# A two-layer kernel on one core: the dense part's squares move from ScalarE to GpSimd, and the hand-written order of pieces is another one

## The chip, the core and the metric

The kernel runs on one core of a Trainium2 chip. The metric is the device time of one execution in microseconds (us), smaller is better. Engines are named as in the profile: PE is TensorE (PEld its weight loads), DVE VectorE, ACT ScalarE, POOL GpSimd, SP SyncE.

## What is computed

The input x is 4 batches of 512 tokens with 128 features, all float32. Two layers, each a LayerNorm and two branches that read it:

```
xn = layernorm(x)
x  = x + L0_attn(xn) + L0_ffn(xn)      # 16 heads, attention over the feature axis;
                                       # 64 experts of width 88, top 8 per token, and 2 shared ones
xn = layernorm(x)
x  = x + L1_attn(xn) + L1_ffn(xn)
```

`L1_attn`: queries and values are relu(xn @ enc); for every token the distances to the 64 tokens behind it are taken per head, the nearest 32 of them are kept with exp(-distance) as weights, and their values are summed; a decoder matmul follows. `L1_ffn`, called the dense part here, is

```
h = xn @ Wfc.T + gate * (xn @ v.T @ fast_b.T @ u.T)     # 128 -> 512
r = max(h, 0)
out = (r * r) @ Wproj.T                                 # 512 -> 128
```

## The kernel before

Every engine has its own program, made of pieces. A piece is a Python generator step; each kind of piece has a letter, and the table `ORDER` writes out for each engine in which order the letters come. `weave` walks through that string. So the order of work on an engine is fixed by hand, and what an engine waits for is set by the semaphores that the pieces name. An engine never passes a piece that waits.

The kinds that matter here:

- `e` on PE: the expert products. The experts' weights are cut into 46 blocks of 128 rows for each batch, 184 in all (n = 0 to 183). Block n fills bank G0 or G1 and bank U0 or U1 (n even or odd), three matmuls each. ACT takes the silu of G; DVE multiplies by U (`S<-S,bank_U`, letter `e` on DVE); the router's weight is put on by DVE for even n (`S<-Rb,bank_G`, letter `m` on DVE, which also frees bank G) and by POOL for odd n (`S<-S,Rb`). `m` on PE is the down product of block n, summed up in bank A.
- ACT makes the high part of each weight block (`Whi`), POOL the low part (`Wlo`).
- `y` and `a`: router and attention of layer 0. `h`: layer 1's head, from the sum of experts (`mo`, copied by ACT from bank A when the 46 down products of a batch are in) through LayerNorm (`yn`), the transposes, the encoder, the metric (`met`) and the lengths of queries and keys (`nmx`, `pq`).
- `d` on PE, `k` (keys, `Ra`) and `n` (near) on ACT: the distances of a group of 64 tokens (8 groups g0 to g7 to a batch) and their exponentials, in tile `Ed`. `k` on DVE: the choosing of the nearest 32 by four rounds of MAX8 and MATCH_REPLACE8. `q` on POOL: subtraction and scaling of what was chosen (`Wk`, `Wm`). `t` on PE: turning that tile (L825), the weighted sum of values, and the decoder. `g` on DVE and ACT: the gathering behind them. In the last batch these matmuls use banks G and U, and the last group is cut in two halves, which DVE finishes alone.
- `f` on PE: one 128-token tile of the dense part's up product, into bank X0, 16 tiles in all (line 670). `f` on ACT (line 1496): relu from the bank into one half of `PR`, then the square in place. `v` on PE (line 682): the down product of the tile, into bank A; it waits on the semaphore `ffsq`. As bank A belongs to the experts until the last batch's sum is copied, all 16 `v` pieces come behind that.

Since there are two halves of `PR`, the relu of tile i waits for the down product of tile i - 2 (`ff2_tile`); since there is one bank X0, the up product of tile i + 1 waits for the relu of tile i.

Of the kernel before, what the change touches and what calls it, by code (L numbers as in the profile page):

```python
# [7 lines left out]
ALU = mybir.AluOpType  # L8
# [41 lines left out]
        "eeemmteeteaeeemmesmtestmesemteeeetmestmmeeeememeeeemmeeeetemeamthmmteeeeeamtheatmaehtaeeeteatemmamee"  # L50
        "meheemhheeeemeemmhehmehaekeekmeedeadeedmememamdeamdeeetfemtdefeemmdeemmfeteetdemeeeeeemteememeetmete"
        "mmetmeetmeeeetmmeeetemtmeeetmeemetmmeeeeeemmtmmthvtvvtfhthfthvhvhfhhhvkddkxdfvfvddtvfvtddtvfdtfvfvfv"
        "vfttvttvtxfttfvttvtvxttxtttttt",
    "dve":
        "yyycyyyyyyyyyyeycyyyyyyeayyyayyyyyyeecyyyyeeyamyeemamaemeemaaeuuaumeuemeuuauuuuemeaemeyeymeeyyyyyyym"
        "eeyyyyyymeeyyymeyeyymeemeyyyyemeeyymeemeemeemeemeemeeeemeeyymeehhyyyymheyyeyyyhhmeeymyeyyhyeyyyyymeh"
        "hehhmeyehmehehahmeahemekkkemkkkkakekekakkmekkekkmgekeamagekmaeekkgkmkegekkemekekmkagekkgemekkekkgkmk"
# [1 line left out]
        "kakaemeakkegkkmeekmekkakkakemeekagkmeekkmgekkkkkmeeakkeakgmeekkgmekgkkemeekkkkmeekmeekgeemeaghhghehh"
        "ameemgeaemgeahgaemeaaemehhhehahmehehmehhemeekkakmekkakkemkkegkkmeekkkekkkmeekmegkekmkegkekmkekgkekme"  # L60
        "gekkmegekkkmegkmekkeemegkkemeekgkkhhhghhghghhhhhhhhhkkkkkkkkkkkkkkkkkkgkkkkkkkkgkkkkgkgkkkkkkgkkgkkk"
        "kkkgkkgg",
    "act":
        "yxxyxyeexexcexxecayaxesyxxseexesaexesxxxeeaxexaeaexxuxeeuxeuuyuxyexeexxeexxxeexexexexexexyexseeyxees"
        "xxxsexeexxxeexexexexexexesxeyxxemeyexexxxexehxeexhehexxoohxeheehhxyexxexhexhhkkveevxknxknenkaeexnaxk"
        "nnxkenxgexeakxnneexxngexeexxexexngnexegxexeaxxexeexegaaxxegxeexexexesxxseexesymesegxxxyexhygexhexhox"
        "eoexexexhheehhxeyxxhhehxekxekexvnkvexnnankaxxnnxkenekkageexxkxenenxgeexxneaxxeexaenaneexxgexxexesxgs"
        "esxeexxgexexexexexesxeexxmgehxeexxghaeaxgeexxhaexeooxhexehaxehheexhxxhhaevxkvkeenkxxnenanekxxknneken"
        "kgfxxkexfenxnexgenexxexeexxexnexgneegxexxeexxeegxxeegxxexeeemgfhghfhohhfhofhhhhkkvnnnnkfnnfvkkfnnnnf"
        "gkkfnnnnkgffnnfffqgfgfqgfgfqgggq",  # L70
    "pool":
        "llylllllalmmlllmaaaclacalamlllmalmllmllmyylmlllmllmllmllmlymlllmmllmlllmlllmllmllmllmlylylmlllmllmll"
        "mhllmlymhlllmllmlmllmlaqllmqallaamqllamplalamlqllmlmlmqlplalmllqmlqlmllmlpmllqllmllmylylplmlhllmlmly"
        "mhllllmmllllaqllaammlaqmlmlalaqlalmlapmllqmlqlmllmllqmplllmlqmllmlmllqllpmlllmlamplhlaaamallaalmlmha"
        "lllmlmllmllqmlllqlmlqmllmlplmqlllmqmlllpmllqmllmqmlllpmmqphhhqqqqqqqq",
# [1791 lines left out]
```

## Time and profile before

| | us |
|---|---|
| median of 3 runs | 679.48 |
| lowest and highest run | 678.58, 680.74 |
| the profiled execution's own time | 678.06 |
| its span in the trace | 676.3 |
| PE, DVE, ACT, POOL busy | 638.7, 545.1, 444.6, 365.4 |

The span is what the trace shows from the first instruction to the last; 1.8 us of the execution's own time lie outside it. The execution that was profiled is 1.4 us quicker than the median run. Busy times of PE are modelled from the starts of its matmuls, since they are pipelined. All times below count from the start of the span.

### The profile page before, as it was taken

What the parts mean: (1) busy time and instruction counts of PE and PEld (TensorE: products, weight loads), DVE (VectorE), ACT (ScalarE), POOL (GpSimd) and SP (SyncE); (2) the same over time, 40 slices, a digit from 0 to 9 for tenths busy, and PEclk for the clock granted to TensorE, in tenths of its full rate; (3) what the DMA queues carried; (4) which work ended last, traced back from release to release, by engine and by line L of the source; (5) the groups of instructions that cost most, each with busy time, mean ns of one, the idle gap of its engine ahead of it and who ended that gap; (6) DMA issues with size and microseconds to landing.
All of it is one profiled execution on the core that took longest, in us unless ns stands there. A gap on an engine that the chain in (4) does not pass through costs nothing.

```text
span 676.3 us, 14256 instructions
## 1 busy us (share of the span) xinstructions
PE 638.7 (94%) x4792; PEld 430.7 (64%) x4792; DVE 545.1 (81%) x2461; ACT 444.6 (66%) x802; POOL 365.4 (54%) x448
## 2 busy tenths in 40 slices
PE   4887999999999999999999999999999999998886
PEld 3544766667656666767567567666567776675675
DVE  5987778645975999997976899965485999967997
ACT  3674454646787957448587786455888956467953
POOL 2278366566462787665452886653763576621220
PEclk9999999999999999999999999999999999999999
DMA  8940000000000000000000000000000000000000
GB/s 297 392 131 1 0 1 0 1 0 1 0 1 1 2 2 1 1 1 1 2 0 2 2 1 2 1 1 1 1 1 1 2 1 1 1 1 17 18 18 17
DMA packets 12968, 15.81 MB, mean 23 GB/s; under 512 B 1728, under 2 KB 10832, under 8 KB 12384
## 3 DMA queue, kind: packets, MB, share of 16 engines
q1 hardware_dynamic: 12896, 14.91, 6.3%
q8 instruction: 38, 0.62, 0.4%
q14 instruction: 34, 0.28, 0.1%
HBM read 13.85 MB, written 1.05 MB: 22 GB/s over the span
## 4 chain that ended last, share of the span: by engine, by line
PE 61%; DVE 24%; ACT 7%; POOL 4%; issue 3%; DMA 0%; DVEq 0%; POOLq 0%; ACTq 0%
PE bank_A L522 17%; PE bank_U L522 14%; PE bank_G L522 14%; PE bank_X L522 14%; DVE Wk L1278 6%; DVE m L1275 5%; DVE S L859 4%; DVE GWk L859 2%; POOL PR L1654 2%; ACT L1350 1%; PE bank_X L531 1%; ACT Ed L1345 1%; PE bank_X L825 1%; ACT PR L1345 1%; ACT L1345 1%
## 5 line engine op out<-in xcount | busy, mean ns | idle before, releaser
L1654 POOL TENSOR_TENSOR Wlo<-Wgu,Whi 128x256 fp32r<-128x256 f32 x184 | 134.9, 743 | 119.5 <-ACT Whi L1345 116.5
L522 PE MATMUL bank_A<-S,WdT 128*128 128x512 f32 x346 | 172.2, 599 | 0.2 <-POOL S L1654 0.2
L1654 POOL TENSOR_TENSOR S<-S,Rb 128x512 f32<-128x512 f32 x84 | 108.6, 1294 | 72.0 <-DVE S L859 71.4
L859 DVE TENSOR_TENSOR S<-S,bank_U 128x512 f32<-128x512 f32 x173 | 116.6, 684 | 37.5 <-PE bank_U L522 23.3
L1345 ACT ACTIVATE Whi<-Wgu 128x256 fp32r<-128x256 f32 x184 | 73.0, 413 | 53.0 <-PE bank_U L522 48.5
L522 PE MATMUL bank_G<-xH,Whi 128*128 128x512 f32 x184 | 94.7, 515 | 8.0 <-POOL Wlo L1654 3.8
L522 PE MATMUL bank_U<-xH,Whi 128*128 128x512 f32 x184 | 93.4, 508 | 1.6 <-DVE wT L859 1.1
L522 PEld LDWEIGHTS bank_A<-S,WdT 128*128 128x128 f32 x346 | 61.7, 189 | 34.6 <-issue 21.4
L1278 DVE MATCH_REPLACE8 Wk<-m,Wk 128x79 f32<-128x79 f32 x384 | 82.2, 226 | 0.0
L1345 ACT ACTIVATE bank_G<-bank_G 128x512 f32<-128x512 f32 x83 | 48.4, 583 | 42.9 <-PE bank_G L522 42.6
L1345 ACT ACTIVATE S<-bank_G 128x512 f32<-128x512 f32 x90 | 53.7, 596 | 34.3 <-PE bank_G L522 27.5
L859 DVE TENSOR_TENSOR S<-Rb,bank_G 128x512 f32<-128x512 f32 x83 | 56.4, 680 | 22.5 <-ACT bank_G L1345 17.6
L522 PE MATMUL bank_U<-xH,Wlo 128*128 128x512 f32 x184 | 72.9, 396 | 0.0
L522 PE MATMUL bank_G<-xH,Wlo 128*128 128x512 f32 x184 | 72.9, 396 | 0.0
L522 PE MATMUL bank_G<-xL,Whi 128*128 128x512 f32 x184 | 72.8, 396 | 0.0
L522 PE MATMUL bank_U<-xL,Whi 128*128 128x512 f32 x184 | 72.7, 395 | 0.0
L1275 DVE MAX8 m<-Wk 128x8 f32<-128x79 f32 x384 | 63.9, 228 | 0.0
L522 PEld LDWEIGHTS bank_G<-xH,Whi 128*128 128x128 f32 x184 | 34.7, 189 | 34.7 <-issue 17.2
L522 PEld LDWEIGHTS bank_U<-xH,Whi 128*128 128x128 f32 x184 | 34.7, 189 | 23.8 <-issue 8.9
L1345 ACT ACT_TABLE_LOAD x38 | 48.8, 1283 | 0.7
L1350 ACT ACT_TABLE_LOAD x35 | 44.9, 1283 | 6.5 <-DVE mv L926 4.4
L1654 POOL TENSOR_TENSOR Wk<-Ed,Wk 128x316 f32<-128x316 f32 x31 | 26.8, 863 | 37.1 <-DVE Wk L1278 36.9
(294 smaller groups left out, 1176.0 us busy)
## 6 DMA issues: line engine op xcount, KB each, us to landing
Wgu<-in_Wgu SPq DMA_DIRECT2D x2, 2048.0 KB, 14.4
xs<-in_x SPq DMA_DIRECT2D x4, 256.0 KB, 6.0
wqk<-in_w_qkv SPq DMA_DIRECT2D x1, 1024.0 KB, 6.9
Wgu<-in_Wgu SPq DMA_DIRECT2D x1, 1024.0 KB, 9.5
out<-xs SPq DMA_DIRECT2D x3, 256.0 KB, 2.3
Wgu<-in_Wgu SPq DMA_DIRECT2D x1, 512.0 KB, 4.7
wout<-in_w_out SPq DMA_DIRECT2D x1, 512.0 KB, 8.1
wvT<-in_wvT SPq DMA_DIRECT2D x1, 512.0 KB, 9.2
```

Of the source, the lines that this page charges most:

```text
L522: return engine.matmul(dst, lhsT, rhs, start=start, stop=stop)
L531: p = engine.transpose(t[0:rows, 128 * i:128 * i + 128], src3[:, i, :], ident)
L825: p = engine.transpose(t[:, 128 * i:128 * i + 128], Wm[s][:, i, :], ident)
L859: return engine.tensor_tensor(dst, a, b, op)
L1275: top[i] = own(engine.max(w8[:, i, 8 * r:8 * r + 8], v[:, i, :]))
L1278: p = engine.match_replace(wk[:, i, :], w8[:, i, 8 * r:8 * r + 8], v[:, i, :], TAKEN)
L1345: return engine.activation(dst, src, f, bias=bias, scale=scale, accum_out=acc)
L1350: engine.preload_act_table_set(LNEXP)
L1654: return engine.tensor_tensor(dst, a, b, op)
```

## The change

Two things. The square of the dense part (`r * r`) is no longer a second ACT instruction behind the relu but a POOL multiply of `PR` with itself, in place, a new kind of piece on POOL with the letter `f`. It waits until ACT's relu has emptied the bank, and counts `ffsq` up. And the strings of `ORDER` for PE, DVE, ACT and POOL are others from the stretch in which batch 0's sum of experts ends; what stands before is the same, and each letter occurs as often as before (POOL's 16 `f` are new).

```diff
@@ ORDER
-        "mmeeeemeeemeeeemyemesmeeseememeemsmeemeeeemeemeeeemmsemeeeememeemeeeemyemeymmeemeeeehymeeeemmmemeeme"
+        "mmemeeeeeememmememyeeeeesmememeeemsmeesmeeemeeeeseeemeeeeememmeememeeeyeeymemeeymeehmmemmemeememehe"
...
@@ scalar_engine, dense(b)
                     if b * NT + i >= 2:
                         sc_.wait_ge("ff2_tile", b * NT + i - 1)
-                    a = emptied(act(r, t[:, :], ACT.Relu), "ff1", b, i)
-                    sc_.wait_ge(*a)
-                    act(r, r, ACT.Square).then_inc(sems("ffsq"), 1)
+                    emptied(act(r, t[:, :], ACT.Relu), "ff1", b, i)
@@ gpsimd_engine
+            def squares(b):
+                for i in range(NT):
+                    r = PR[:, 512 * (i % 2):512 * (i % 2) + 512]
+                    yield
+                    po.wait_ge(empty(bank("ff1", b, i)), nth("ff1", b, i) + 1)
+                    tt(r, r, r, ALU.mult).then_inc(sems("ffsq"), 1)
...
-            weave("pool", c=zeros(), l=splits(), m=tiles(), y=every(route), a=every(attend), h=every(head), q=every(weights), p=adds())
+            weave("pool", c=zeros(), l=splits(), m=tiles(), y=every(route), a=every(attend), h=every(head), q=every(weights), p=adds(), f=every(squares))
```

**Place 1, DVE, near the end of batch 0's experts** (blocks 24 and 25). `GWk`, `sfc` and `m8r` are tiles of batch 1's router. Before:

```order
L1043 TENSOR_REDUCE GWk<-GWk 128x32 [waits dve]
L863 TENSOR_SCALAR GWk<-GWk 128x32 [waits dve]
L859 TENSOR_TENSOR S<-Rb,bank_G 128x512 [waits down,silu]
L859 TENSOR_TENSOR S<-S,bank_U 128x512 [waits U0_filled,G0_emptied]
L859 TENSOR_TENSOR S<-S,bank_U 128x512 [waits U1_filled,G1_emptied]
L859 TENSOR_TENSOR sfc<-sfc,GWk 128x256 [waits dve]
```

After:

```order
L1043 TENSOR_REDUCE GWk<-GWk 128x32 [waits dve]
L863 TENSOR_SCALAR GWk<-GWk 128x32 [waits dve]
L859 TENSOR_TENSOR sfc<-sfc,GWk 128x256 [waits dve]
L859 TENSOR_TENSOR S<-Rb,bank_G 128x512 [waits down,silu]
L859 TENSOR_TENSOR S<-S,bank_U 128x512 [waits U0_filled,G0_emptied]
```

The router's `sfc` multiply has moved ahead of the weight piece that frees bank G0.

**Place 2, PE, the end of the last batch's experts.** `bank_A<-S,WdT` is a down product, L825 turns the last batch but one's group, `cst,mo` are the transposes of the finished sum. Before:

```order
L522 MATMUL bank_A<-S,WdT 128x512 [waits U0_emptied]
L522 MATMUL bank_A<-S,WdT 128x512 [waits tw_p]
L825 MATMUL bank_X<-cst,Wm 128x128 [waits chosen_p,X2_emptied]
L825 MATMUL bank_X<-cst,Wm 128x128 x3
L531 MATMUL bank_X<-cst,mo 128x128 [waits mo,X1_emptied]
```

After:

```order
L522 MATMUL bank_A<-S,WdT 128x512 [waits U0_emptied]
L825 MATMUL bank_X<-cst,Wm 128x128 [waits chosen_p,X2_emptied]
L825 MATMUL bank_X<-cst,Wm 128x128 x3
L522 MATMUL bank_A<-S,WdT 128x512 [waits tw_p]
L522 MATMUL bank_X<-wT,V 32x32 [waits X2_emptied]
L522 MATMUL bank_X<-wT,V 32x32 x15
L531 MATMUL bank_X<-cst,mo 128x128 [waits mo,X1_emptied]
```

The turn stands before the last down product now, and the sum of values that belongs to it before the transposes.

**Place 3, ACT and POOL, the last batch's first groups.** ACT after the change, from the first keys to the second group's near piece (before, the near pieces of g0 and g1 stood directly one behind the other, behind the `V` copy, and only then came a `Ra` and a dense tile):

```order
L1345 ACTIVATE Ed<-bank_G 128x316 [waits looked,G0_filled]
L1345 ACTIVATE Ed<-Ed,cst 128x316 [waits G0_emptied]
L1345 ACTIVATE Ed<-Ed 128x316 [waits act] x2
L1345 ACTIVATE Ra<-Pk 16x316
L1345 ACTIVATE V<-bank_U 128x512 [waits U1_filled]
L1345 ACTIVATE Ra<-Pk 16x316 [waits G1_filled]
L1345 ACTIVATE PR<-bank_X 128x512 [waits ff2_tile,X0_filled]
L1345 ACTIVATE Ra<-Pk 16x316 [waits G0_filled]
L1345 ACTIVATE PR<-bank_X 128x512 [waits ff2_tile,X0_filled]
L1345 ACTIVATE Ed<-bank_G 128x316 [waits looked]
```

POOL after the change in the same stretch, with the squares:

```order
L1652 TENSOR_TENSOR hg<-hg,kp 128x128 [waits X2_emptied]
L1652 TENSOR_TENSOR PR<-PR 128x512 [waits X0_emptied] x2
L1732 COPY kp<-kp 128x63 [waits X1_emptied]
L1652 TENSOR_TENSOR PR<-PR 128x512 [waits X0_emptied]
L1652 TENSOR_TENSOR hg<-hg,hf 128x512 [waits hf_inv]
L1652 TENSOR_TENSOR PR<-PR 128x512 [waits X0_emptied]
L1652 TENSOR_TENSOR hg<-hf,kp 128x512 [waits U0_emptied]
L1652 TENSOR_TENSOR PR<-PR 128x512 [waits X0_emptied] x2
L1652 TENSOR_TENSOR Wk<-Ed,Wk 128x316 [waits taken]
```

On ACT six other pieces now stand between the near pieces of g0 and g1, and on POOL the squares stand between the head's multiplies and the groups' `Wk` and `Wm`.

## Rows read from the trace of the kernel before

**Rows 1.** The page: busy time by engine, and the chain that ended last.

```profile
PE 638.7 (94%) x4792; PEld 430.7 (64%) x4792; DVE 545.1 (81%) x2461; ACT 444.6 (66%) x802; POOL 365.4 (54%) x448
PE 61%; DVE 24%; ACT 7%; POOL 4%; issue 3%; DMA 0%; DVEq 0%; POOLq 0%; ACTq 0%
```

**Rows 2.** Busy time of each engine in three stretches.

```profile
core 0: us, PE busy (x) PEld busy (x) DVE busy (x) ACT busy (x) POOL busy (x), PEclk, DMA share, GB/s
105.00:596.60 491.60, 487.36 (x3456) 321.42 (x3457) 401.49 (x1800) 334.63 (x595) 295.83 (x362) 1.00 0.01 1
596.60:620.30 23.70, 22.04 (x257) 16.41 (x255) 12.40 (x44) 18.20 (x37) 4.80 (x6) 1.00 0.04 13
620.30:671.60 51.30, 41.84 (x671) 34.96 (x669) 50.86 (x414) 35.64 (x72) 11.01 (x14) 0.97 0.06 16
```

**Rows 3.** Timeline of PE: start, duration, line, tiles [idle before].

```profile
104.89 0.50 PE L522 MATMUL bank_G<-xH,Whi 128*128 128x512 f32 x1 [1.16 <-DVE S L859]
```

**Rows 4.** Timeline of DVE around the same moment.

```profile
104.16 0.68 DVE L859 TENSOR_TENSOR S<-Rb,bank_G 128x512 f32<-128x512 f32 x1
...
106.07 0.42 DVE L859 TENSOR_TENSOR sfc<-sfc,GWk 128x256 f32<-128x256 f32 x1
```

**Rows 5.** The chain that ended last: start, duration, what.

```profile
592.26 0.70 PE bank_U L522 x3
...
596.65 0.61 ACT mo L1345
...
598.02 0.89 PE bank_A L522 x8
...
601.48 0.44 PE bank_X L825 x4
601.92 0.89 PE bank_X L522 x8
602.81 0.45 PE bank_X L531 x4
...
606.45 0.61 ACT Qb L1345
607.06 0.15 ACT hb L1345
...
611.98 1.13 PE bank_U L522 x2
...
615.09 1.09 PE bank_A L522 x8
...
617.41 0.87 PE bank_G L522 x33
```

**Rows 6.** Timeline of DVE in the last batch.

```profile
601.32 1.12 DVE L864 TENSOR_SCALAR mo<-xs,mv,ln 128x128 f32<-128x128 f32 x4
...
612.42 0.51 DVE L864 TENSOR_SCALAR mk<-kp,met 128x575 f32<-128x575 f32 x1
...
620.36 0.67 DVE L1275 MAX8 m<-Ed 128x8 f32<-128x79 f32 x4 [2.59 <-ACT Ed L1345]
...
626.40 0.66 DVE L1275 MAX8 m<-Ed 128x8 f32<-128x79 f32 x4
...
671.17 0.32 DVE L859 TENSOR_TENSOR Wm<-Wk,sm 128x158 f32<-128x158 f32 x1
```

**Rows 7.** Timeline of ACT in the last batch.

```profile
618.30 0.43 ACT L1345 ACTIVATE Ed<-bank_G 128x316 f32<-128x316 f32 x1 [0.26 <-PE bank_G L522]
...
619.36 0.96 ACT L1345 ACTIVATE Ed<-Ed 128x316 f32<-128x316 f32 x2
```

**Rows 8.** Instructions on tile PR: nanoseconds, shortest, median and longest; first and last start.

```profile
L1345 ACT ACTIVATE PR<-PR x20: 629/631/634, 46.8 to 662.0; 128x512 f32<-128x512 f32 x20
L1654 POOL TENSOR_TENSOR PR<-PR x4: 1042/1042/1043, 47.5 to 481.7; 128x512 f32<-128x512 f32 x4
L1654 POOL TENSOR_TENSOR PR<-PR,z x4: 1271/1287/1602, 48.6 to 482.8; 128x512 f32<-128x512 f32 x4
L1654 POOL TENSOR_TENSOR z<-PR x4: 1310/1318/1769, 52.7 to 486.1; 128x512 f32<-128x512 f32 x4
```

**Rows 9.** Groups of POOL's instructions in the last 79 us: count, busy us, mean ns.

```profile
L1654 POOL TENSOR_TENSOR Wk<-Ed,Wk 128x316 f32<-128x316 f32 x8 | 6.9, 858 | 32.6 <-DVE Wk L1278 32.6
L1654 POOL TENSOR_TENSOR Wm<-Wk,sm 128x316 f32<-128x316 f32 x8 | 5.7, 714 | 3.9 <-PE bank_U L825 3.4
```

More of the change, by code:

```diff
@@ L45 @@
         "yeyeyeeemeeaeaemaayeeaseeeseeameesmaeesemmmemmeeeemeemumaeeaeeaumeeeueaueemyeeymmmymeeeeemmeeemmeeee"
-        "mmeeeemeeemeeeemyemesmeeseememeemsmeemeeeemeemeeeemmsemeeeememeemeeeemyemeymmeemeeeehymeeeemmmemeeme"
-        "mheeheeeehmeehhmmeeymeemhmhmeeheeeakeekadeademdeeemeaemmdeadeematmeeteadmeedememmtedteeeemeetmmeeete"
-        "mtmmeteemmeetemmmeeeemteaeeetmmtameaeeeteetememameemmseeeeesmeeseeetseeemhtmytmeeetymmtemhteheyeeemm"
-        "emeheemememhheeemyehemhmheaeeaeeeemkdekedaedeemeadeammdaedateeeteemmmmedemmeetmmeeetdeeeemmeateamema"
@@ L50 @@
[L50 to L53, printed above, removed]
+        "mmemeeeeeememmememyeeeeesmememeeemsmeesmeeemeeeeseeemeeeeememmeememeeeyeeymemeeymeehmemmemeemememehe"
+        "ememheememeeeehmeehhemeyememahheaehmeeeeedkdaeedemmmmaeeedaedemkateeeatdmedemtmetememeemdeeeemteteee"
@@ new lines @@
+        "tmmemmeetemteemememeatmeeeeateateetmmteemeeeeemmeemtemeeatmmseeseeeheemsmtesemeyteymemteeeyehmetheee"
+        "mheemmhheeemmmmeeeheehmeemeheeeeykedmadeadeaeeamdaemdkatmaeeedeetemmmmeemdmtmeetmeeeeeedeemaemaeeeam"
+        "tmememeaeteeeemsmeeetseemmsteetmsmeemeetmeeememeeeetmemetemathmatmeeteaetamheehteaeeetmaetaemememmht"
+        "eeeemhheeemmemaheehmaheememedeedeeeaedeemmeedkmmdeemadkeetfmefeetdfmmeetmeeeteedememmteeeemmmeeeemme"
+        "temteeteetemeemmeeemteeeeteetemetmmeeeetmmtmmmtmthvtvthfhfthvhhvvhhhfvddfkdvfxvkdfdtvtdvtdtdfvfvfvfv"
@@ L54 @@
+        "vttxttfvtfvfttvttvtvxttxtttttt",
     "dve":
         "yyycyyyyyyyyyyeycyyyyyyeayyyayyyyyyeecyyyyeeyamyeemamaemeemaaeuuaumeuemeuuauuuuemeaemeyeymeeyyyyyyym"
-        "eeyyyyyymeeyyymeyeyymeemeyyyyemeeyymeemeemeemeemeemeeeemeeyymeehhyyyymheyyeyyyhhmeeymyeyyhyeyyyyymeh"
-        "hehhmeyehmehehahmeahemekkkemkkkkakekekakkmekkekkmgekeamagekmaeekkgkmkegekkemekekmkagekkgemekkekkgkmk"
-        "keeakmeekmkgeayeyyekemeeygymeehghhmehhgyyyemgyyyyyeyyyyyyyhemeyeyyymyeyhhhemhehyhaemeehmeahehmekkkkk"
@@ L59 @@
[L59 to L62, printed above, removed]
-    "act":
[L64 to L70, printed above, removed]
+        "eeyyyyyyymeyemyeyemeyeymeeyyyymeyeymeemeemeemeemeemeeeemeyyyeyymhhehyyyehyymehemeyeyyyymeyeyyyhymeey"
@@ new lines @@
+        "mehhyhhaehmheemhheeahmekkkekmkkkakkekkeameekkkgkkkamaeemkgekemeagkkmkeekkgkkemeeagkkmeekkkmgeekmkgak"
+        "ekkkmegekemkeekgeayyeymeeyymgehehhmehyyhgemygeyeyhmyyyyyyeyyehmheyhyyeymhyeyyehmyehehmeheyhameakkkkk"
+        "kakkaemeakkekkkmeekmgakkekgaemeeakmekekkkkmkegkkeakmeekameekmekkgkmkgeekekkmekkemekgkeeegmahhagehghh"
+        "emeegmeaeagahmeeagmeaehhahmehehmehehhmheemeakekkkkmeekkkakkmekkkmgeekemkkekkegkmkeekkmeekkmgekkemgek"
+        "kemkkeekgmekemgekkekgkmeekkgmeekgkghhhhhghghhhhhhhhhkkkkkkkkkkkkkkkkkkkkkkgkkkgkkkkkggkkkkkkkgkkkgkk"
@@ new lines @@
+        "kkkkkggg",
+    "act":
+        "yxxyxyeexexcexxecayaxesyxxseexesaexesxxxeeaxexaeaexxuxeeuxeuuyuxyexeexxeexxxeexexeexexxexeyxeeyxesex"
+        "xxsexsexexxeexexexxxeexeesexxyxeyexmexxeehexxexexhexehxoexexhoexhxhyehexhxehhkexexkknennknxaekxvaexn"
+        "nkevxknegexannxxkgeexenexxeexgenxnxxeegeaxxxeeaxxeeaxgeexgexexexxexexegmsexxeysesxxsexeyghxyexexhexe"
+        "hooxheehexxxehhxxeexhexehxhkexykvkennknaxnaknxnevenkxaegkkexxxeenngexxnexeaxexxaeeaxnxneexexexgexsee"
+        "xxesgxesexexexxexexgexsemxghxaeehegaxxexegxahxexeohexexhxaeehaxhoexahexhhekkxknxekenxnkexnxeeknnknxv"
+        "evexxfgkefxnnexegxexnexexneexxneexxegxxegexexexexexexgexegeegmghfhfhhhohoffhhhhkkfnnkvkfkfnnnnkvgnnn"
+        "nnnkkgffnnffnnfqfgfgffqgfgfqgggq",
@@ L71 @@
     "pool":
[L72 to L75, printed above, removed]
+        "llylllllalmmlllmaaaclacalamlllmalmllmllmyylmlllmllmllmlmlmylllmllmlmlllmlllmlmllllmlmlyllylmllmllmlm"
@@ L76 @@
+        "llmlhllmyllhmllmllmllmlqaqlmaallaalmlqmallpmlaqlmllqmllmalpmllqlmlqlmlpllmmqllllmlllmyylllpmlmhlmlll"
+        "mllhmlylmlllaqllaammamlqmalqalllamlallmlpqllmlmqllmlmllqlpmmllllmllqlmqlplmmlalllmpaaalalhamllamallh"
+        "mlmlllmlllmqmllqlflfmlmlqllpmlqmllmllqlmllmqmplllmlllqmmpmqpffhfhfhffqqfqfqffqffqffqq",
 }
```

## Prediction

> **What bounds the kernel now.** I read the page first. PE is busy for 94% of the span, and the chain that ended last is PE for 61%, DVE for 24% and ACT for 7% [rows 1]. Then the busy times by stretch [rows 2], which show three kinds of time. From 105 us to the end of the experts (596.6 us) PE is busy for 487.36 of 491.60 us: here the kernel is as long as PE's own work, and the order can take away at most the 4.24 us in which PE stands still. From 596.6 to 620.3 us, the last batch's head, no engine is full: the chain walks from the copy of the sum (596.65 us) through LayerNorm, encoder and metric to the first distances at 617.41 us [rows 5]. From 620.3 to 671.6 us DVE is busy for 50.86 of 51.30 us: it chooses the nearest 32 of the last batch's groups from its first MAX8 at 620.36 us to the last `Wm`, which ends at 671.49 us [rows 6]. Behind it lie 4.8 us to the end of the span, which neither order changes.
>
> So the time is the end of PE's work, plus the head, plus DVE's choosing. The squares are only worth what they do to one of these. Three of the 16 dense tiles go up before the last sum is copied, as before, the other 13 behind it, and all 16 down products lie behind it.
>
> **The change, part by part.** All times are set against the profiled execution's own 678.06 us; it lies 1.42 us under the median of the runs (679.48 us), and I carry the difference over to the median.
>
> (1) *The squares themselves.* ACT gives up 16 instructions of 0.631 us, 10.1 us; POOL takes on 16 of 1.042 us, which is what its multiply of one half of PR with itself takes in layer 0 [rows 8], 16.7 us. POOL is busy for 4.80 of 23.70 us and 11.01 of 51.30 us in the two last stretches [rows 2], so it has the room. A tile's way from relu to down product gets 0.41 us longer. Neither is on the path by itself: between 620 and 671 us the dense part runs beside the choosing, where ACT is busy for 35.64 of 51.30 us. Cost by itself: 0. If the cover were gone, the 0.41 us of each of the 13 late tiles would count, 5.3 us.
>
> (2) *The first moved rows* (place 1). PE waits 1.16 us at 104.89 us for the weight piece that frees bank G0 [rows 3]; that piece runs on DVE from 104.16 to 104.84 us, at the end of a run of router work, and the router's `sfc` multiply of 0.42 us comes at 106.07 us [rows 4]. In the new order `sfc` stands ahead of the weight piece, and PE's own order up to this point is as it was. So PE waits that much longer: +0.45 us with the gap between instructions.
>
> (3) *The rest of the expert stretch.* The letters are the same, so PE's work is the same. Of the waits between 105 and 596.6 us, 4.24 us in all [rows 2], the new order may lose all or none, and may make new ones; between these ends no row decides. One thing speaks for a slight gain. I counted in both orders the work that PE has between the filling of U(n) and the down product n, with 0.70 us for three expert matmuls and 0.87 for a down product [rows 5]: the shortest such distance is 1.6 us before and 2.3 us after, so DVE and POOL have more room. I take -0.5 us, with -4.2 and +4 as bounds (as much in new waits as there is now).
>
> (4) *The end of the experts* (place 2). The turn of a group, 0.44 us [rows 5], stands before the last down product instead of behind it, so the sum is complete 0.44 us later: +0.44 us. In exchange its sum of values lies in the shadow of ACT's copy.
>
> (5) *The head.* I followed the new order from the copy of the sum (596.65 + 0.61 = 597.26 us) on, with the durations of the rows. Before, the transposes of `yn` start at 602.81 us [rows 5], though DVE is done with it at 602.44 us [rows 6], since a turn and a dense tile stand in front; the dense tile is now behind them: -0.3 us. The encoder and ksq follow at that distance. Then `hb` starts at once, while before a `Qb` of 0.61 us stood in front of it, ending at 607.06 us [rows 5]; it now has to wait for PE's metric matmul, and I come to 0.67 us earlier altogether. The metric chain keeps this up to 611.98 us (now 611.3). Between 615.09 and 617.41 us PE had a dense down product and the values, 2.32 us [rows 5]; the new order has a dense tile up and one down there, 0.89 + 0.89 us and some 0.2 for the changes of shape: -0.3 us. Together the first distances are ready 0.95 us earlier, counted from the copy: -0.95 us.
>
> (6) *The choosing.* A near piece takes from 618.30 to 620.32 us, 2.02 us [rows 7], and the groups follow each other on DVE at 626.40 - 620.36 = 6.04 us [rows 6]. Before, g1's near piece came directly behind g0's. Now two relus, three `Ra` and the `V` copy stand between them, and the second relu waits for an up product that stands on PE behind a down product. Following PE and ACT row by row, I get the end of g1's near piece 6.3 to 6.4 us behind the end of g0's, so DVE waits about 0.3 us: +0.3 us. The later groups have some 4 us and more to spare. DVE's pieces themselves are as many as before; one gather moves from before the last `Wm` to behind it, but the last turn waits for that gather (it frees the bank), so nothing is won there: 0.
>
> Sum: 0.45 - 0.5 + 0.44 - 0.95 + 0.3 = -0.26 us. Against the profiled 678.06 us this is 677.8, against the median **679.2 us**.
>
> **The rivals.** The measurement can tell a change of about 0.3% from none, which is 2.0 us here: 677.4 and 681.5 us are the borders.
>
> *(A) As reckoned, or a little beside it*, within the border: 679.2 us, by itself from 677.6 to 681.0.
>
> *(B) The new order also clears the expert stretch.* Everything that was idle there, 4.24 us instead of 0.5, is gone, and g1 comes in time (-0.3): 679.2 - 3.7 - 0.3 = 675.2 us. For it speaks the wider distance of (3). Against it: the waits are short and scattered, and the only one of over 1 us gets longer by (2).
>
> *(C) The dense part comes too late for the last groups: slower.* In the new POOL order, the squares of tiles 10 to 15 stand behind `Wk` and `Wm` of groups 3, 4 and 5, two instructions of 0.858 and 0.714 us [rows 9], and these in turn wait for DVE's fourth round and for a turn on PE. On PE the down products that wait for these squares stand in front of the turn and the sum of values of the next group. The narrowest place by my following is the sum of values of g3: it is ready some 0.1 us before DVE, in its order, comes to gather it behind g5. Each us by which squares are late beyond that is a us of DVE. A whole round of up product, relu, square and down product is 0.89 + 0.6 + 1.04 + 0.89 = 3.4 us: 682.6 us. It decides from about 2 us of lateness on. Against it: POOL has 40 us without work in that stretch, and most of the waits are short of the gather by microseconds.
>
> *(D) POOL and DVE hold each other up.* POOL's multiplies of 128x512 mostly take 1.27 to 1.32 us, but single ones 1.60 and 1.77 us [rows 8]: 0.3 to 0.45 us longer, beside DVE work. A square that begins at the metric's `nmx` and `mk` (0.51 us, [rows 6]) could hold `nmx` up by as much as its own 1.04 us, of which 0.6 lie in front of PE's own arrival: +0.4 us, 679.6 us. MAX8 keeps its 0.66 us beside POOL's `Wk` [rows 6], so the choosing is not touched. The Trainium skill ("SBUF — State Buffer", on the shared port pair) says that a DVE instruction in a two-port mode or with two SBUF inputs and a GpSimd instruction exclude each other for their whole length, while one with a single SBUF input and no such mode doesn't; by that rule, too, it is `nmx` and `mk` that are exposed and MAX8 that isn't. The longest single rows of POOL agree in kind.
>
> **How the numbers follow.** A 0.44, B 0.27, C 0.19, D 0.10 (D stays within the border). So faster 0.27, same 0.54, slower 0.19. The likeliest is A: 679.2 us. The range takes in most of B and C, whose own times are 675.2 and 682.6 us: 675.6 to 682.4 us.
>
> **What the profile after would show.** (1) 16 POOL rows PR<-PR more, of 1.04 us, none of ACT's squares, and POOL busy near 382 us. (2) The wait at 105 us at 1.5 to 1.7 us. (3) PE busy for all but 3 to 5 us between there and the last down product. (5) From the start of the last copy of `mo` to DVE's first MAX8 of the last batch 22.8 us instead of 23.7. (6) A wait of 0.1 to 0.6 us of DVE for `Ed` at g1, and none after it; 51.1 us and this wait from the first MAX8 to the last `Wm`. The prediction is wrong where PE has new waits in the expert stretch of over 2 us, where DVE waits for gathers in the last 50 us (C), or where the sum is copied over 2 us sooner (B).

## The result: slower by 0.46%

| | before | after |
|---|---|---|
| median of the runs | 679.17 us (18 runs, 677.99 to 680.79) | 682.75 us (18 runs, 679.88 to 685.62) |
| the profiled execution: own time, span | 678.06, 676.3 us | 681.87, 680.1 us |

The ratio of the runs is 1.0046, with a 95% interval of 1.0034 to 1.0058: 3.1 us slower (2.3 to 3.9), where 679.2 us and no measurable change were forecast. Ratios compare runs on the same chip at the same time; measured beside the later kernels, before has medians of 678.8 to 679.9 us, so kernels of different groups are compared below by their ratios. One execution of e17_best_products in another state, 1050.95 us at a mean granted clock of 0.56, is left out.

**The profile after.** First the page's busy times and chain, which answer to [rows 1]:

```profile
PE 642.7 (95%) x4792; PEld 436.1 (64%) x4792; DVE 550.7 (81%) x2461; ACT 435.7 (64%) x787; POOL 383.3 (56%) x464
PE 73%; DVE 18%; ACT 4%; issue 3%; POOL 1%; DMA 0%; DVEq 0%; POOLq 0%; ACTq 0%
```

Then the busy times by stretch, as in [rows 2] (behind the bare numbers stand the granted clock, the DMA share and GB/s):

```profile
105.00:596.60 491.60, 485.13 (x3452) 321.96 (x3452) 406.29 (x1802) 333.74 (x594) 299.25 (x364) 1.00 0.01 1
597.00:620.30 23.30, 20.16 (x184) 14.81 (x187) 12.55 (x43) 14.77 (x29) 6.58 (x9) 0.93 0.04 13
620.30:671.60 51.30, 45.32 (x700) 37.77 (x692) 48.11 (x392) 30.14 (x62) 23.46 (x26) 0.93 0.05 15
```

In the same 491.60 us PE now stands still for 6.47 us instead of 4.24. But these two windows don't hold the same waits: the change's has its 1.62 us at 105 us in it, and before's begins just behind its 1.16 us. Taken from the end of PE's work ahead of that wait (103.73 us before, 105.05 us after the change) to the last copy of `mo`, the same stretch is, before and after:

```profile
103.73:596.60 492.87, 487.47 (x3456) 321.53 (x3457) 402.69 (x1803) 334.63 (x595) 295.83 (x362) 1.00 0.01 1
```

```profile
105.05:598.50 493.45, 486.99 (x3462) 322.69 (x3465) 406.97 (x1805) 334.33 (x595) 300.91 (x366) 1.00 0.00 1
```

So the standstills grew from 5.40 to 6.46 us, and the stretch by 0.6 us, at the full granted clock in both. Of the 5.40 us, 2.5 were three waits of over 0.5 us and 2.9 shorter ones; after the change 5.7 are four long waits and only 0.7 are short ones. The timeline of PE says where; each row ends with the idle time before it and what ended it:

```profile
106.67 0.50 PE L522 MATMUL bank_G<-xH,Whi 128*128 128x512 f32 x1 [1.62 <-DVE S L859]
...
247.68 0.50 PE L522 MATMUL bank_G<-xH,Whi 128*128 128x512 f32 x1 [1.73 <-DVE S L859]
...
359.19 0.50 PE L522 MATMUL bank_G<-xH,Whi 128*128 128x512 f32 x1 [1.84 <-DVE S L859]
...
604.43 0.85 PE L531 MATMUL bank_X<-cst,mo 128*128 128x128 f32 x3 [1.88 <-DVE mo L864]
```

Before had 1.16 us [rows 3] and 0.67 us at the first two of these and nothing at the third. Before the transposes of `yn` PE did not stand still in the kernel before, since a turn and a dense tile filled the time [rows 5]. The other end points, from the timelines of ACT (the last copy of `mo`) and DVE (first MAX8 and last `Wm` of the last batch):

```profile
598.56 0.60 ACT L1345 ACTIVATE mo<-bank_A 128x512 f32<-128x512 f32 x1 [0.26 <-PE bank_A L522]
```

```profile
623.00 0.67 DVE L1275 MAX8 m<-Ed 128x8 f32<-128x79 f32 x4 [2.26 <-ACT Ed L1345]
...
674.33 0.32 DVE L859 TENSOR_TENSOR Wm<-Wk,sm 128x158 f32<-128x158 f32 x1
```

Against [rows 5, 6] the copy of `mo` is 1.91 us later, from there to MAX8 it takes 24.44 us instead of 23.71, the choosing 51.33 instead of 50.81, and what lies behind it 5.77 instead of 5.13 (680.1 - 674.33 and 676.3 - 671.17). These add up to the spans' 3.8 us. But 1.3 us of the first item come before anything has moved, in the first 94 us: 1.0 us of it by 24 us, the rest about a stretch at half the granted clock at 58 us (last section) that before's profile has not. One profile can't say what is chance. So I used the profiles of all kernels below, which share long stretches of one order or the other.

The lower clock is part of the difference, and not all of it. Beside the later kernels before ran 127 times, and the median of its runs' mean granted clocks is 0.991; the change's is 0.987. At 0.993 before took 678.5 us (median of 31 runs) and the change 680.0 (2 runs), at 0.991 679.4 (39 runs) and 681.1 (2 runs): at an equal clock some 1.5 to 1.7 us remain. The split is rough, since a stretch at half clock costs nothing where PE isn't what bounds.

### The profile page after: what moved, and what is told of

Same layout as the page of the kernel before. It is cut to its first block, busy times and chain, and to the rows that moved or that the text cites. A ratio compares the mean times of both kernels' runs of the same rounds, so it can differ in the third digit from the quotient of the medians.

```text
span 680.1 us, 14248 instructions
## 1 busy us (share of the span) xinstructions
PE 642.7 (95%) x4792; PEld 436.1 (64%) x4792; DVE 550.7 (81%) x2461; ACT 435.7 (64%) x787; POOL 383.3 (56%) x464
## 4 chain that ended last, share of the span: by engine, by line
PE 73%; DVE 18%; ACT 4%; issue 3%; POOL 1%; DMA 0%; DVEq 0%; POOLq 0%; ACTq 0%
PE bank_A L522 19%; PE bank_G L522 17%; PE bank_U L522 17%; PE bank_X L522 17%; DVE Wk L1278 5%; DVE m L1275 4%; DVE S L859 2%; PE bank_X L825 1%; PE bank_X L531 1%; DVE GWk L859 1%; ACT L1350 1%; DVE xn L864 1%; ACT Ed L1345 1%; DMA xs<-in_x 0%; POOL z L1652 0%
## 5 line engine op out<-in xcount | busy, mean ns | idle before, releaser
L522 PE MATMUL bank_G<-xH,Whi 128*128 128x512 f32 x184 | 97.1, 528 | 10.6 <-DVE S L859 5.2
L522 PE MATMUL bank_U<-xH,Whi 128*128 128x512 f32 x184 | 95.9, 521 | 1.1 <-DVE wT L859 1.1
L522 PEld LDWEIGHTS bank_U<-xL,Whi 128*128 128x128 f32 x184 | 35.0, 190 | 15.6 <-issue 11.2
```

Of the source, the lines that this page charges most:

```text
L522: return engine.matmul(dst, lhsT, rhs, start=start, stop=stop)
```

## Why DVE's product is late: La and rq

All three waits shown of the expert stretch are for the same instruction, DVE's `S<-Rb,bank_G`, the product that frees bank G0. DVE's timeline ahead of the last one:

```profile
354.40 0.34 DVE L867 SCALAR_TENSOR_TENSOR PQ<-PQ,cst,bank_X 64x128 fp32r<-64x128 f32 x1 [0.41 <-ACT PQ L1345]
354.77 3.76 DVE L859 TENSOR_TENSOR La<-PQ,cst 64x256 fp32r<-64x256 f32 x1
358.46 0.67 DVE L859 TENSOR_TENSOR S<-Rb,bank_G 128x512 f32<-128x512 f32 x1
```

and POOL's at the same time:

```profile
354.93 0.74 POOL L1652 TENSOR_TENSOR Wlo<-Wgu,Whi 128x256 fp32r<-128x256 f32 x1
355.62 1.27 POOL L1652 TENSOR_TENSOR S<-S,Rb 128x512 f32<-128x512 f32 x1
356.85 1.41 POOL L1652 TENSOR_TENSOR Wlo<-Wgu,Whi 128x256 fp32r<-128x256 f32 x2
```

`La` takes 3.76 us; the same 64x256 product takes 0.46 us at 202.5 us in before's trace, and 1.37 us at this place in before. It ends 0.3 us behind the end of POOL's run of four instructions without a gap (354.93 to 358.26 us). At 244.5 us, ahead of the wait of 1.73 us, it is the router's small rows (0.15 to 0.23 us each when undisturbed), each of which ends within 0.03 us of the end of one POOL instruction (245.09, 246.32 and 247.00 us):

```profile
244.52 0.60 DVE L859 TENSOR_TENSOR rq<-rq 128x8 f32<-128x8 f32 x1
245.15 1.19 DVE L867 SCALAR_TENSOR_TENSOR rq<-rq 128x8 f32<-128x8 f32 x1
246.38 0.65 DVE L859 TENSOR_TENSOR rq<-rq,tsc 128x8 f32<-128x8 f32 x1
246.95 0.67 DVE L859 TENSOR_TENSOR S<-Rb,bank_G 128x512 f32<-128x512 f32 x1
```

## The experiments

Names with "act" or "order" have the squares on ScalarE, `e8`, `e16` and `e17` too; the others on GpSimd. "Copy to MAX8" is from the start of the last copy of `mo` to the first MAX8 of the last batch, "choosing" from there to the start of the last `Wm`, both from the kernel's profile, in us.

| kernel | median (runs) | ratio to before, 95% | copy to MAX8 | choosing |
|---|---|---|---|---|
| e1_squares | 682.60 (6) | 1.0047 [1.0029, 1.0064] | 24.18 | 52.34 |
| e2_order | 682.86 (6) | 1.0050 [1.0030, 1.0070] | 23.02 | 52.00 |
| e3_mid_after_tail_before | 685.43 (6) | 1.0095 [1.0076, 1.0115] | 24.18 | 52.34 |
| e4_mid_before_tail_after | 682.90 (6) | 1.0063 [1.0043, 1.0084] | 24.43 | 51.33 |
| e5_fill | 683.08 (12) | 1.0036 [1.0020, 1.0052] | 22.85 | 51.34 |
| e6_near | 683.20 (6) | 1.0053 [1.0034, 1.0072] | 22.89 | 51.08 |
| e7_squares_placed | 681.18 (12) | 1.0017 [1.0002, 1.0031] | 24.16 | 50.83 |
| e8_gap | 681.17 (12) | 1.0026 [1.0012, 1.0040] | 25.38 | 50.82 |
| e9_weights_first | 680.81 (12) | 1.0016 [1.0003, 1.0029] | 22.88 | 51.33 |
| e10_weights_near | 680.30 (12) | 1.0011 [1.0000, 1.0022] | 24.46 | 51.09 |
| e11_weights_act | 681.29 (12) | 1.0021 [1.0005, 1.0036] | 23.00 | 51.99 |
| e12_best_act | 679.86 (12) | 1.0008 [0.9996, 1.0020] | 22.95 | 50.61 |
| e13_best_pool | 680.43 (12) | 1.0011 [0.9997, 1.0026] | 23.42 | 51.10 |
| e14_short_pool | 679.51 (10) | 1.0007 [0.9989, 1.0025] | 24.46 | 51.33 |
| e15_product_first | 678.57 (11) | 1.0000 [0.9987, 1.0012] | 22.89 | 51.12 |
| e16_before_products | 679.85 (12) | 1.0018 [1.0007, 1.0028] | 23.71 | 50.82 |
| e17_best_products | 678.95 (11) | 1.0007 [0.9993, 1.0021] | 22.95 | 50.62 |

### The two halves of the change, and the order cut in two

**e1_squares.** before's strings, with `squares` on POOL and sixteen `f` put into POOL's string:

```
-"... lllmlmllmllqmlllqlmlqm ... lllpmmqphhhqqqqqqqq"
+"... lllmlmllmllqmlllfqlfmlqm ... lllpmmqfpfhfhhfqffqfqfqffqffqffqq"
```

> Only the squares move: the order of before on every engine, and 16 squares put into GpSimd's order where its timeline of before had room (two in the expert stretch, fourteen in the tail). Theory 1 (the new order loses the time): within 1 us of before, mean granted clock .995 or more, PE standing still 4 to 5 us between 105 and 596.6 us. Theory 2 (the squares on GpSimd lose it, by their 0.41 us more of latency each or by standing beside DVE): 2 to 3.5 us above before, as the whole change.

**e2_order.** The new strings without the `f` of POOL; `dense` makes the squares on ACT as before.

> Only the order moves: the new order on every engine with the squares left on ScalarE directly behind their relus. Theory 1: 2 to 3.5 us above before, with PE's new waits at 106.7, 247.7, 359.2 and 604.4 us and a mean granted clock under .992. Theory 2: within 1 us of before.

**e3_mid_after_tail_before** and **e4_mid_before_tail_after.** Each engine's string up to its last product of the experts from one order, the rest from the other.

> Squares on GpSimd, the new order up to the last product of the experts, then before's order. If the expert stretch loses the time (its new waits, 2.2 us): about +2 us against before, the last copy of mo near 598.5 us, and from there to the first MAX8 of the last batch 23.7 us as before. If the head loses it (1.88 us of standstill of PE before the transposes of yn, and half the clock for 3.4 us behind it): within 1 us of before.

> Squares on GpSimd, before's order up to the last product of the experts, then the new order. If the expert stretch loses the time: within 1 us of before, or 0.7 us under it. If the head loses it: +1.5 to +3 us, with the standstill of 1.9 us before the transposes of yn and the granted clock at half behind it.

Each half alone was as slow as both: neither theory 1 nor theory 2 as I had put them. That the new order alone is as slow as the change (e2_order, 1.0050) shows that the change doesn't need the squares on GpSimd to lose its time. e1_squares loses by the places that I gave the squares. In the expert stretch PE waits 0.67 us at 543.9 us for a POOL product behind a square. In the timelines of the last batch two squares wait on POOL behind a `Wm` that waits for a turn, and PE stands still for them with the turn of a later group queued behind; first PE, then POOL:

```profile
660.80 0.46 PE L522 MATMUL bank_A<-WpT,PR 128*128 128x128 f32 x2 [2.03 <-POOL PR L1652]
```

```profile
658.94 0.71 POOL L1652 TENSOR_TENSOR Wm<-Wk,sm 128x316 f32<-128x316 f32 x1 [3.39 <-PE bank_U L825]
659.62 2.04 POOL L1652 TENSOR_TENSOR PR<-PR 128x512 f32<-128x512 f32 x2
```

That is rival C with all its links, but in the old order; the choosing of e1_squares grew by 1.53 us. e3 has the same tail (52.34) and the new middle besides, which is the slowest of all. e4 is no clean cut: the last turn now stood before the last down product, waited 0.56 us for DVE and made the sum late. What the pair does show is that the new middle costs: e3 and e1_squares differ in it alone, by 2.8 us of median.

**e7_squares_placed.** The two squares in the expert stretch moved to where POOL waits 3.85 us for DVE, one more square ahead of group 5's `Wk` (against e1_squares):

```
-"... lllfqlfmlqm ... qmlllpmllqmllmqmlllpmmqfpfhfhhfqffqfqfqffqffqffqq"
+"... lllqlmlqm ... qmlllpmllqmllffmqmlllpmmqfpfhfhhfqffqfqfqfffqfqffqq"
```

> As e1_squares (before's order, squares on GpSimd), but the two squares in the expert stretch stand where GpSimd waited 3.9 us for VectorE, and one more square stands ahead of group 5's Wk. If the squares cost nothing by themselves and e1_squares lost by their places (0.95 us at 542 us, 1.5 us of VectorE's waiting at group 6): within 0.7 us of before. If it is the squares themselves (0.41 us more of latency each, or the neighbourhood of VectorE): still 2 us or more above before.

The copy of `mo` starts at 596.70 us (before: 596.65 [rows 5]), and the choosing takes 50.83 us: nothing lost there. In the head it is 0.45 us more, because PE waits for the square of the third tile with the next turn queued behind:

```profile
600.83 0.94 PE L522 MATMUL bank_A<-WpT,PR 128*128 128x128 f32 x6 [0.39 <-POOL PR L1652]
```

By the runs it is 0.1 to 2.1 us slower than before. In before's order the squares cost about 0.5 us by the profile; the runs allow more. They say nothing of the new order, for which e9_weights_first and e11_weights_act stand below.

### The head

**e5_fill.** PE's and ACT's tails of the change (and on POOL the tail's first square one place sooner, `"qpffh"` as `"qfpfh"`):

```
-pe  "thvtvthfhfthvhhvvhhhf"    act "gmghfhfhhhohoff"
+pe  "thvtvtfhvhfthhhvvhhhf"    act "gmfghhfhhhohoff"
```

> The whole change, but in the head ScalarE takes the third dense tile's relu directly behind the copy of mo, TensorE puts the next dense tile in front of the transposes of yn and a down product behind them. If the 1.88 us in which TensorE stands still there, and the half clock behind it, are what the head loses: no stretch at half clock between 600 and 612 us, 23.0 us from the start of the last copy of mo to the first MAX8 instead of 24.44, and 1 to 1.5 us under the change. If that fall of the clock has nothing to do with the standstill: the same time as the change, within 0.5 us.

**e8_gap.** before's PE: `"thvtvvtfhthfthv"` became `"thvtvthfhtvfthv"`.

> The kernel before, squares on ScalarE, with one thing done to it: in the head TensorE has the transposes of yn ahead of the dense tile and of one down product, as in the new order, so that it stands still some 1.5 us before them. If such a standstill makes the granted clock fall on the chain of the head: the mean granted clock 0.002 to 0.004 lower than before's and 0.7 to 1.5 us slower. If the standstill costs nothing since VectorE's yn is not ready sooner: within 0.3 us of before.

**e6_near.** ACT: `"kkfnnkvkfkfnnnn"` became `"kkfnnnnkvkfkfnn"`.

> The whole change, but ScalarE makes the exponentials of group 1 of the last batch directly behind those of group 0, in front of two relus, the Ra rows and the V copy. If group 1's lateness costs what the trace of the change shows (6.76 us between the first two groups' last steps instead of 6.03): 50.6 us from the first MAX8 to the last Wm instead of 51.33, and 0.6 to 0.8 us under the change. If the later groups only become late in its place: no change, or up to 1 us slower.

e5_fill's profile did what the first theory said (0.80 us of standstill instead of 1.88, the clock at 1.00 in the head, 22.85 us), but its runs are no faster than the change's within their intervals: the ratios differ by 0.7 us, and anything from 0.7 us slower to 2.0 us faster fits. So no gain is shown, and the head's standstill isn't shown to be a large part. e8_gap was confounded: moving the sum of values behind the encoder made `kp` wait 1.39 us for POOL's `hg`. PE stood still for 1.31 us before the transposes without a fall of the clock, and the mean granted clock of its runs was as high as before's. e6_near took the 0.73 us at group 1 and gave 0.48 us back at group 6 (51.08 us of choosing instead of 51.33); its runs show no gain.

### The products that PE waits for

**e9_weights_first.** Three neighbours exchanged in DVE's order of the change. The last of them, as the order shows it:

```
+L859 TENSOR_TENSOR S<-Rb,bank_G 128x512
 L867 SCALAR_TENSOR_TENSOR PQ<-PQ,cst,bank_X 64x128
 L859 TENSOR_TENSOR La<-PQ,cst 64x256
-L859 TENSOR_TENSOR S<-Rb,bank_G 128x512
 L859 TENSOR_TENSOR S<-S,bank_U 128x512
```

> The whole change, with three neighbours exchanged in VectorE's order: the product with Rb that frees bank G0 (S<-Rb,bank_G) stands ahead of sfc at 105 us, of the four rq rows at 244.5 us and of La at 354.8 us. Theory: the change loses in the expert stretch, where this product stands behind small VectorE rows that GpSimd's run of instructions stretches (La 3.76 us, three rq rows 0.60, 1.19 and 0.65), and TensorE stands still for it (1.62, 1.73 and 1.84 us). Then the waits at 247.7 and 359.2 us are gone, the one at 106.7 is 1.16 us again, La stays stretched, and the run is 3 to 4.5 us under the change: 678.3 to 679.8 us. Rival: TensorE only waits somewhere else for the same, or the loss is in the tail: within 1 us of the change.

**e10_weights_near** and **e11_weights_act** are e9_weights_first with e6_near's ACT string, and with the squares on ACT.

> e9_weights_first with e6_near's order on ScalarE as well (group 1's exponentials directly behind group 0's). In e6_near's profile this took the 0.73 us of VectorE's waiting at group 1 and gave 0.48 us back at group 6. Expected: 0 to 0.7 us under e9_weights_first, last Wm 50.6 to 51.1 us behind the first MAX8. Rival: the later groups lose as much, no difference.

> e9_weights_first with the squares back on ScalarE. If the squares on GpSimd cost nothing in the new order: within 0.7 us of e9_weights_first. If they cost what e7_squares_placed showed in the head of before's order (0.5 us in the profile) or more: 0.5 to 1.5 us under it. If GpSimd's squares are a gain (ScalarE has less in front of group 1's exponentials, which were 1.4 us late in e2_order and 0.7 in the change): up to 0.7 us above it.

About 2 us came back (1.0046 to 1.0016), two thirds of the loss, with three exchanges, of which two shortened a wait. The third only moved its wait. In e9_weights_first's timeline of PE the 1.73 us at 247.7 us are gone, and two instructions on stands

```profile
249.55 0.50 PE L522 MATMUL bank_U<-xH,Whi 128*128 128x512 f32 x1 [1.80 <-DVE S L859]
```

because the next product, `S<-S,bank_U`, was still behind the `rq` rows. At 359.1 us 0.74 us of 1.84 are left (and 0.40 us new behind it), at 106.7 us 1.15 of 1.62. e11_weights_act and e9_weights_first are the same within their intervals: in the new order no cost of the squares on GpSimd is shown, to about 1.5 us either way (with ACT's squares group 1 is later, 51.99 us of choosing against 51.33).

**e14_short_pool.** Nothing is moved; POOL's instructions beside `La` are cut short. The kernel leaves out all but 8 columns of them, so it no longer computes the same result; it is there for its times alone:

```
-tt(Wlo[w][:, :], Wgu[:, n % NF, :], Whi[w][:, :].bitcast(F), ALU.subtract)
+c = slice(0, 8 if 112 <= n <= 114 else 256)
+tt(Wlo[w][:, c], Wgu[:, n % NF, c], Whi[w][:, c].bitcast(F), ALU.subtract)
...
-tt(s, s, Rb[k][:, :], ALU.mult)
+c = slice(0, 8 if weight_count(n) == 52 else 512)
+tt(s[:, c], s[:, c], Rb[k][:, c], ALU.mult)
```

> The whole change, with the four GpSimd instructions that run beside La at 354.8 us cut short: the low parts of weight blocks 112 to 114 and one product with Rb are made for 8 columns only, so that they are left out of the result otherwise. Theory: La takes 3.76 us because VectorE's instruction, which reads two SBUF tiles, waits out GpSimd's run from 354.93 to 358.26 us; then it takes 0.5 to 1 us here, TensorE's wait of 1.84 us at 359.2 us is gone, and the run is 1.5 to 3 us under the change. Rival: La is long for a reason of its own (its operands, the bank it waits for): it keeps 3 us or more and so does TensorE's wait.

Its timelines of DVE and of POOL at that place:

```profile
357.46 0.50 DVE L859 TENSOR_TENSOR La<-PQ,cst 64x256 fp32r<-64x256 f32 x1
357.88 0.67 DVE L859 TENSOR_TENSOR S<-Rb,bank_G 128x512 f32<-128x512 f32 x1
```

```profile
357.60 0.42 POOL L1652 TENSOR_TENSOR Wlo<-Wgu,Whi 128x8 fp32r<-128x8 f32 x1
357.99 0.20 POOL L1652 TENSOR_TENSOR S<-S,Rb 128x8 f32<-128x8 f32 x1
358.15 0.20 POOL L1652 TENSOR_TENSOR Wlo<-Wgu,Whi 128x8 fp32r<-128x8 f32 x1
```

`La` is back at 0.50 us, PE doesn't wait there any more, and the ratio to before falls from 1.0046 to 1.0007, by some 2.6 us (1.2 to 4.1 by the intervals). The stretch of `La` by POOL's run is shown. The fall may be more than the 1.84 us of the wait; the last section has what the rest may be. With this one wait gone the kernel is level with before within the interval, though the other waits of the new order are still there.

**e15_product_first.** e10_weights_near with DVE's `"kkkmaaeem"` as `"kkkmeaaem"`.

> e10_weights_near, with the product S<-S,bank_U of the next block also ahead of the four rq rows at 244.5 us. In e9_weights_first the wait of 1.73 us at 247.7 us only moved two instructions on (1.80 us at 249.6 us), since this product still stood behind the rq rows. Theory: the wait falls under 0.6 us and the run is 1 to 1.5 us under e10_weights_near. Rival: the stretched rq rows make the next product late in the same way, and nothing is gained.

The wait at 247 to 250 us is gone, and nothing as long took its place in the middle (the longest left are 1.15 us at 106.1 us and 0.78 us at 357.9 us). The kernel is equal to before: 1.0000, from 0.9987 to 1.0012. Against e10_weights_near (1.0011) this last exchange gave 0.7 us, which the intervals don't tell from nothing. So the whole loss comes back when four products of DVE and group 1's exponentials are moved, with the squares on GpSimd and the rest of the new order as it is.

### Is there a faster one?

**e12_best_act** has before's order into the head, then ACT `"hhhohoff"` for `"hohhfhof"`, PE `"fthvhhvhhhfvdd"` and the new tail with e6_near's exchange. **e13_best_pool** has the squares on POOL besides.

> Before's order up to the head of the last batch, squares on ScalarE, and from the encoder on the new order's head and choosing, with group 1's exponentials directly behind group 0's. If the new head is worth what the profiles of the kernels with it show (22.9 to 23.0 us from the last copy of mo to the first MAX8 instead of 23.7, 51.1 instead of 50.8 us of choosing) and the expert stretch of before has none of the new waits: 0.4 to 0.8 us under before. If that head brings its falls of the clock along (3 of 7 profiles): no better than before, up to 0.7 us above.

> e12_best_act with the squares on GpSimd, placed as in e7_squares_placed in the expert stretch. If the squares cost 0.5 us in the head as in e7_squares_placed, where two down products stand early on TensorE: 0.5 us above e12_best_act. If ScalarE's gain (no square in front of the exponentials) makes up for it: the same within 0.3 us.

**e16_before_products** and **e17_best_products**: before and e12_best_act, with DVE's `"yyyyyymee"` as `"yymeeyyyy"` at 102 us and `"eamage"` as `"emaeag"` at 244 us.

> The kernel before, with the products that free TensorE's banks put ahead of small VectorE rows at its own two waits: at 102.3 us (GWk rows) and at 244.6 us (rq rows). If what the experiments on the change showed holds for before as well: the waits of 1.16 us at 104.9 us and 0.67 us at 247.8 us are gone, and the run is 1 to 2 us under before. Rival: TensorE waits for the next product instead, as in e9_weights_first at 249.6 us: within 0.5 us of before.

> e12_best_act (before's middle, new head and choosing, squares on ScalarE) with the same two exchanges as e16_before_products. 1 to 2 us under e12_best_act, and 0.5 to 2 us under before. Rival: as above, no gain over e12_best_act.

No kernel beat before. e12_best_act's profile has all it should (22.95 and 50.61 us), but the 1.0 us by which its last `Wm` is earlier is lost behind it, where its clock was at half from 667.1 us on (before's from 674.0 us), and its runs show no gain. In e16_before_products the rival came: both waits went away and came back one link on, here in PE's timeline

```profile
111.43 0.50 PE L522 MATMUL bank_G<-xH,Whi 128*128 128x512 f32 x1 [1.86 <-DVE S L859]
```

where the product stands behind the MAX8 rows of the router, which had been pushed back. An exchange need not give anything: the rows that the product overtakes still have to run ahead of the next one. My reading, which no run isolates, is that it gives something only where DVE's rows are stretched or DVE has time to spare behind them.

## Why the prediction was wrong, point by point

(1) *The squares, cost 0.* Not contradicted in the new order (e9 against e11, within about 1.5 us; 16 POOL rows more, of 1.04 us, POOL busy for 383.3 us). In before's order they would have cost some 0.5 us, and 3 us with careless places (e1_squares), the price of rival C.

(2) *Wait at 105 us.* Right: 1.62 us, 1.5 to 1.7 forecast.

(3) *The rest of the expert stretch, -0.5 us.* **This step failed.** I had counted what PE has between U(n) and the down product n, at nominal durations. In part that was right: the waits of under 0.5 us shrank from 2.9 to 0.7 us. But new standstills of 0.55 us at 131.6 us, 1.06 at 247.7 and 1.84 at 359.2 came in, 3.45 us, which the sum had left to its upper bound of +4. The two long ones come from the other release, of bank G0 by DVE's weighted product, and from what stands ahead of it on DVE at its stretched length (`La` 3.76 us instead of 0.46). Counted as idle time of PE between the same points, the change lost 1.06 us, 0.46 of it step (2), so this step measured +0.6 instead of -0.5 us. By its length the stretch grew by 0.6 us with steps (2) and (4) in it, which leaves -0.3 us (busy times of PE are modelled, so the two differ). So in an execution at full clock the new standstills only ate what the wider distances gave. (Rival B also counts the 1.16 us at 104.89 us among the waits of 4.24 us, whose window begins behind it.)

The other part of the failure is a term that the sum did not have at all, the granted clock. Every duration in it was taken at full clock, and behind the 1.84 us PE ran at half clock in four of five profiles, for 1.25 us more. e14_short_pool, without that one wait, gives back 2.6 us, and e15_product_first with group 1's exchange 3.1 us. An estimate from the profiles: 0.46 (2), -0.3 (3), 0.8 x 1.25 for the clock there, 0.45 (4), -0.75 (5), 0.4 x 1.5 for the clock in the head, 0.52 (6) and 0.1 behind the choosing are 2.1 us, of the 2.3 to 3.9 us measured. The shares 0.8 and 0.4 come from five and ten profiles, and what is left of the difference stays open.

(4) *Turn ahead of the last down product.* Right: the turn starts at 597.05 us and the down product behind it at 597.50, 0.45 us later (0.44 forecast).

(5) *Head, -0.95 us.* Right in mechanism and size where the clock stayed up: 22.88 to 23.02 us in e2, e6, e9, e11 and e15, -0.7 to -0.8 us. In the change's own profile it is +0.73 us. I had seen that the dense tile went behind the transposes, and not that PE would stand still for 1.88 us in its place, and that in four profiles of ten, this one among them, it would run at half clock behind that.

(6) *Group 1 late by 0.3 us.* Mis-sized: 0.73 us (6.76 us between the first two groups' last steps, 6.03 undisturbed), of which DVE's own wait is 0.62 us:

```profile
629.75 0.67 DVE L1275 MAX8 m<-Ed 128x8 f32<-128x79 f32 x4 [0.62 <-ACT Ed L1345]
```

ACT's second relu waits 0.76 us for its up product. Of the 0.73 us, 0.52 are in the choosing's length. No later wait: rival C's mechanism is absent. The last `Wm` to the end, which neither order was to change, did change a little: from the start of `Wm` it is 5.1 us in before, e1, e3, e7 and e16, and 5.2 to 5.3 us in e5, e6, e9 and e15, which have the new tail and whose clock falls to half as late behind `Wm` (2.8 to 3.2 us). In the change's profile, where it falls 1.8 us behind it, it is 5.77.

Rival D had the right mechanism and too small a place. `mk` beside a square does take 1.30 us instead of 0.51 [rows 6], but the price was paid at `La` and `rq`, in the stretch where PE bounds. The Trainium skill ("SBUF — State Buffer", "SBUF: two separate sides") says that a VectorE instruction with two SBUF inputs and a GpSimd one that reads SBUF lock each other out for a whole instruction. e14_short_pool agrees that the two hold each other up, and each stretched `rq` row ends with one GpSimd instruction. But `La` waited out four GpSimd instructions, not one.

## What to carry to other kernels

When an order is rewritten, look at what stands on VectorE ahead of each product that frees a bank of TensorE, and take small instructions with two SBUF inputs at the length that they have beside GpSimd's work (here up to 8 times their shortest). Move the product ahead only together with the next ones in the chain, and see whether the wait is gone or has moved on (e9 and e16 against e15). Judge two halves of a change by runs, read each profile's clock before explaining a difference of a microsecond, and start two windows that are to be compared at the same event, not at the same time.
